# A graph-attention layer with its groups written out, its inputs laid out by partitions and its weights split by chunks

## What is computed

```python
h = jnp.maximum(_layernorm(x, axis=-1), 0.0)            # x: (64, 128, 384)
q = _heads(h @ Wq + bq)                                  # W: (384, 384), 6 heads of 64
k = _heads(h @ Wk + bk)
v = _heads(h @ Wv + bv)
scores = jnp.einsum('bhqd,bhkd->bhqk', q, k) / np.sqrt(HEAD_SIZE)
bias = jnp.where(adj, 0.0, NEG)[:, None]                 # adj: (64, 128, 128) booleans
probs = jax.nn.softmax(scores + bias, axis=-1)
ctx = jnp.einsum('bhqk,bhkd->bhqd', probs, v)
x = x + (ctx.transpose(0, 2, 1, 3).reshape(...) @ Wf + bf)
```

## Time and profile before

| | |
|---|---|
| median of three timed runs | 483.15 us (482.45 to 484.91) |
| the profiled execution's own time | 482.62 us |
| its span in the profile | 480.8 us |
| PE busy | 461.3 us, 96% |
| DVE busy | 366.4 us, 76% |
| ACT busy | 361.6 us, 75% |
| POOL busy | 304.3 us, 63% |
| moved by DMA | 79.76 MB |

### The profile page before, as it was taken

How to read it: one execution, slowest core, us unless ns; L and a number is a source line. 1 busy time by engine, 2 the same in 40 slices (tenths; PEclk the granted TensorE clock), 3 DMA queues, 4 the chain that set the end, 5 groups by cost and what they waited for, 6 DMA issues and landing times.

```text
span 480.8 us, 12961 instructions
## 1 busy us (share of the span) xinstructions
PE 461.3 (96%) x4451; PEld 272.9 (57%) x4451; DVE 366.4 (76%) x734; ACT 361.6 (75%) x806; POOL 304.3 (63%) x305
## 2 busy tenths in 40 slices
PE   6888989999999999999999999999999999999985
PEld 4644555646556564655656465565646565565643
DVE  3989878977769587776959777695977769477953
ACT  3478887877787887777788787778868778767850
POOL 4447665767757576776757677665767766654663
PEclk9999999999999999999999999999999999999999
DMA  7847597988989798686868869697997969756796
GB/s 245 177 66 152 108 191 158 154 189 135 221 118 205 166 168 207 129 221 131 202 144 178 191 131 219 132 204 149 172 198 127 222 116 165 168 117 147 144 188 182
DMA packets 231430, 79.76 MB, mean 166 GB/s; under 512 B 213331, under 2 KB 231382, under 8 KB 231382
## 3 DMA queue, kind: packets, MB, share of 16 engines
q1 hardware_dynamic: 214144, 66.09, 70.6%
q10 hardware_dynamic: 17238, 13.05, 10.4%
HBM read 16.19 MB, written 12.58 MB: 60 GB/s over the span
## 4 chain that ended last, share of the span: by engine, by line
PE 79%; DMA 7%; SPq 6%; DVE 3%; issue 2%; POOL 2%; ACT 1%; ACTq 0%; DVEq 0%
PE ps_proj L755 23%; PE ps_proj L757 22%; PE ps_proj L756 22%; PE ps_scores L828 6%; DMA ht_parts<-h_parts 3%; DMA ct_parts<-ctx_parts 2%; PE ps_ctx L755 2%; PE ps_ctx L756 2%; PE ps_ctx L757 2%; SPq L375 2%; SPq L359 2%; SPq L367 1%; DMA x_sb<-in_x 1%; DVE w_lo L690 1%; SPq L349 1%
## 5 line engine op out<-in xcount | busy, mean ns | idle before, releaser
L427 POOL TENSOR_TENSOR probs_parts<-probs,probs_parts 128x768 f16<-128x768 f32 x64 | 106.1, 1657 | 31.2 <-ACT probs_parts L519 30.3
L511 ACT ACTIVATE probs<-masked,neg_max 128x128 f32<-128x128 f32 x384 | 118.5, 390 | 0.2
L755 PE MATMUL ps_proj<-ht_parts,w_hi 128*128 128x512 f16 (+1 forms) x315 | 112.0, 361 | 5.3 <-DMA ht_parts<-h_parts 5.0
L756 PE MATMUL ps_proj<-ht_parts,w_hi 128*128 128x512 f16 (+1 forms) x315 | 111.9, 361 | 0.0
L757 PE MATMUL ps_proj<-ht_parts,w_lo 128*128 128x512 f16 (+1 forms) x315 | 111.9, 361 | 0.0
L491 ACT ACTIVATE qkt_hi<-ps_proj,bias_qk 128x512 f16<-128x512 f32 x96 | 65.3, 683 | 58.9 <-PE ps_proj L757 58.1
L412 POOL TENSOR_TENSOR h_parts<-h_sb,h_parts 128x384 f16<-128x384 f32 x64 | 58.9, 928 | 59.5 <-ACT h_sb L482 59.5
L590 DVE SCALAR_TENSOR_TENSOR qkt_lo<-ps_proj,bias_qk,qkt_hi 128x512 f16<-128x512 f32 x96 | 70.4, 741 | 29.7 <-ACT qkt_hi L491 29.7
L433 POOL TENSOR_TENSOR ctx_parts<-ctx_sb,ctx_parts 128x384 f16<-128x384 f32 x64 | 58.6, 915 | 51.6 <-ACT ctx_parts L525 51.1
L633 DVE SCALAR_TENSOR_TENSOR masked<-ps_scores,score_unscale,mask 128x384 f32<-128x384 f32 x128 | 72.6, 609 | 6.5 <-PE ps_scores L828 6.4
L422 POOL TENSOR_TENSOR x_bf<-x_sb,b_out 128x384 f32<-128x384 f32 x64 | 63.2, 999 | 9.8 <-DVE y_sb L663 8.8
(11 more groups left out here) (73 smaller groups left out, 887.6 us busy)
## 6 DMA issues: line engine op xcount, KB each, us to landing
y<-y_sb SPq DMA_DIRECT2D x64, 192.0 KB, 2.6
x_sb<-in_x ACTq DMA_DIRECT2D x60, 192.0 KB, 3.0
adj_sb<-in_adj ACTq DMA_DIRECT2D x16, 64.0 KB, 3.8
ht_parts<-h_parts SPq DMA_TRANSPOSE x64, 2.9
pt_parts<-probs_parts SPq DMA_TRANSPOSE x64, 4.0
ct_parts<-ctx_parts SPq DMA_TRANSPOSE x64, 2.5
x_sb<-in_x SPq DMA_DIRECT2D x4, 192.0 KB, 4.3
w_raw<-in_L_gnn_Wq SPq DMA_DIRECT2D x1, 576.0 KB, 7.8
```

The source lines that it names most:

```text
L427: nc.gpsimd.tensor_tensor(probs_parts[b][:, 1, :], probs[b % 2][:], probs_parts[b][:, 0, :], ALU.subtract).then_inc(probs_split, 1)
L511: last = nc.scalar.activation(probs[b % 2][:, u * N:(u + 1) * N], masked[b % 2][:, u, :], ACT.Exp, bias=neg_max[b % 2][:, u:u + 1])
L755: nc.tensor.matmul(to, a_hi, b_hi, start=first, stop=False)
L756: nc.tensor.matmul(to, a_hi, b_lo, start=False, stop=False)
```

## The change

All sixteen groups are written out; there is no loop on the engines. The tables of groups 0, 1, 14 and 15 have other turns (`TURNS` is the same), so the order changes in the first and last groups. The biases come from the host as one array of 128 by 3 by 3, so that one DMA brings them to their columns and PE no longer turns them; the mask's input is laid out by partitions, in runs of 512 B instead of 128 B. `bf` and the masks of groups 0 and 1 are loaded on SP's queue behind the weights, no longer on ACT's. `w_hi` and `w_lo` of the first three weights are written in three chunks, each with its own count of a semaphore, and PE waits chunk by chunk. `first_q` has its loops over chunks and tiles exchanged. `keep_busy` is called once with 20 instead of with 8 and 4.

```diff
-def run_turns(engine, stages):
-    todo = turns_of(stages)
-    for turn, stage, group, item in todo:
-        if turn < LOOP_TURNS[0]:
-            stages[stage](group, item, 0)
-    with engine.Fori(0, REPS) as i:
...
+def run_turns(stages):
+    for turn, stage, group, item in turns_of(stages):
+        stages[stage](group, item, 0)
...
     1: {
-        "statistics": (-65207, -58743, -57083, -46447), "aggregate": (-27850,), "inverse_deviation": (-60088,),
+        "statistics": (-28344, -20747, -20493, -13756), "aggregate": (-13197,), "inverse_deviation": (-20677,),
...
+            sp.dma_start(bf_rows[:], bf.partition_broadcast(P)).then_inc(bf_loaded, 16)
+            for n in range(2):
+                sp.dma_start(adj_sb[n][:], adj[n, :, :, :]).then_inc(adj_loaded[n], 16)
...
-            for n, bias in enumerate((bq, bk, bv)):
-                act.dma_start(bias_line[:, n, :], bias.rearrange("(o n) -> o n", o=1)).then_inc(bias_loaded, 16)
-            act.dma_start(bf_rows[:], bf.partition_broadcast(P)).then_inc(bf_loaded, 16)
-            act.wait_ge(consts_set, 5)
+            act.dma_start(bias_raw[:], biases).then_inc(bias_loaded, 16)
+            act.wait_ge(consts_set, 4)
             nc.scalar.activation(table_loader[:], eps[:], ACT.Exp)
-            load_mask(0, 0, 0)
-            act.wait_ge(bias_copied, 1)
...
-            load_mask(1, 0, 0)
+            for c in range(C):
+                weight_hi(1, slice(c, c + 1))
             for b in range(B):
                 load(1, b, 0)
-            weight_hi(1)
...
-                if group == 0 and j == 1:
-                    weight_hi(2)
+                if group == 0 and j == 2:
+                    for c in range(C):
+                        weight_hi(2, slice(c, c + 1))
...
-                if j == 0:
-                    scale(2)
...
                 if j == 2:
+                    for c in range(C):
+                        split_weight(2, slice(c, c + 1), c + 1)
+                if j == 5:
                     reduce_rows(3)
...
-            dve.wait_ge(bias_turned, 1)
-            nc.vector.tensor_copy(bias_raw[:], bias_turned_in.rearrange("p (n c) -> p n c", n=3))\
-                .then_inc(bias_copied, 1)
...
-            nc.vector.tensor_scalar(w_hi[0][:], w_raw[0][:], w_scale[:, 0:1], None, ALU.mult)\
-                .then_inc(w_hi_ready[0], 1)
-            split_weight(0)
+            for c in range(C):
+                chunk = slice(c, c + 1)
+                nc.vector.tensor_scalar(w_hi[0][:, chunk, :], w_raw[0][:, chunk, :], w_scale[:, 0:1], None, ALU.mult)\
+                    .then_inc(w_hi_ready[0], 1)
+                split_weight(0, chunk, c + 1)
...
             reduce_rows(2)
-            split_weight(1)
-            run_turns(dve, {
+            for c in range(C):
+                split_weight(1, slice(c, c + 1), c + 1)
+            scale(2)
...
                     pe.wait_ge(h_transposed[b], 16)
-                    if b == 0:
-                        pe.wait_ge(w_split, 1)
                     tokens = slice(b * N, (b + 1) * N)
-                    for j in range(C):
-                        at = slice(j * P, (j + 1) * P)
-                        for c in range(C):
+                    for c in range(C):
+                        if b == 0:
+                            pe.wait_ge(w_split[0], c + 1)
+                        for j in range(C):
+                            at = slice(j * P, (j + 1) * P)
...
-                    if b == 0:
+                    if b == 1:
                         sum_rows(1)
...
-            pe.wait_ge(consts_set, 5)
-            turn_biases()
-            keep_busy(8)
+            pe.wait_ge(consts_set, 4)
+            keep_busy(20)
             pe.wait_ge(bias_summed, 1)
             sum_rows(0)
             project_bias()
-            keep_busy(4)
```

More of the change, by code:

```diff
@@ L293, in build @@
         w_hi_ready = [sem(f"w_hi_ready{n}") for n in range(4)]
-        w_split = sem("w_split")
+        w_split = [sem(f"w_split{n}") for n in range(4)]
         biases_ready = sem("biases_ready")
@@ L502, in values_hi @@
                                      ACT.Copy).then_inc(v_hi_ready, 1)
-                if group == 0 and b == 1:
+                if group == 0 and b == B - 1:
                     weight_hi(3)
@@ L622, in values_lo @@
                                         v_hi[group % 2][:, b, :, 0:D], ALU.subtract).then_inc(v_split, 1)
-                if group == 0:
-                    between_first_values(b)
+                if group == 0 and b == 2:
+                    scale(3)
+                    dve.wait_ge(scale_step, 4 * SCALE_STEPS)
+                    nc.vector.tensor_tensor(y_unscale[:], w_unscale[:, 2:3], w_unscale[:, 3:4], ALU.mult)\
+                        .then_inc(unscales_ready, 1)
             def mask_scores(g, b, i):
@@ L787, in project_qk @@
                         pe.wait_ge(h_transposed[b], by_group(group, i))
-                if group == 0 and j == C:
-                    pe.wait_ge(w_split, 2)
                 ps = free_bank("project_qk", group, j, i)
@@ L793, in project_qk @@
                 for c in range(C):
+                    if group == 0 and j == C:
+                        pe.wait_ge(w_split[1], c + 1)
                     last = three_passes(ps[:], w_hi[w][:, c, at], w_lo[w][:, c, at], hi[:, c, :], lo[:, c, :],
@@ L806, in project_v @@
                 for c in range(C):
+                    if group == 0 and b == 0:
+                        pe.wait_ge(w_split[2], c + 1)
                     last = three_passes(ps[:, 0:H], hi[:, c, at], lo[:, c, at], w_hi[2][:, c, :], w_lo[2][:, c, :],
@@ L809, in project_v @@
                 last.then_inc(v_projected, 1)
+                if group == 0 and b == 2:
+                    sum_rows(3)
             def scores(g, pair, i):
@@ L870, in sum_rows @@
                 last.then_inc(rows_summed, 1)
-            def turn_biases():
-                pe.wait_ge(bias_loaded, 3 * 16)
-                for n in range(3):
-                    for c in range(C):
-                        k = C * n + c
-                        last = nc.tensor.matmul(bias_turned_in[:, k:k + 1], bias_line[:, n, c * P:(c + 1) * P], one[:],
-                                                start=True, stop=True)
-                last.then_inc(bias_turned, 1)
             def keep_busy(times):
@@ L900, in _, with laid_out @@
             project_bias()
-            keep_busy(4)
-            run_turns(pe, {
+            run_turns({
                 "project_qk": project_qk, "project_v": project_v, "scores": scores, "weigh_values": weigh_values,
                 "project_out": project_out})
-_INS = ["x", "adj", "L0_gnn_Wq", "L0_gnn_bq", "L0_gnn_Wk", "L0_gnn_bk", "L0_gnn_Wv", "L0_gnn_bv", "L0_gnn_Wf",
-        "L0_gnn_bf"]
+def laid_out(inputs, np):
+    adj = np.asarray(inputs["adj"]).reshape(GROUPS, B, N, N).transpose(0, 2, 1, 3)
+    biases = np.stack([np.asarray(inputs[f"L0_gnn_b{w}"]) for w in "qkv"]).reshape(3, C, P).transpose(2, 0, 1)
+    yield "x", inputs["x"]
+    yield "adj", adj
+    for w in "qkvf":
+        yield f"W{w}", inputs[f"L0_gnn_W{w}"]
+    yield "biases", biases
+    yield "bf", inputs["L0_gnn_bf"]
 def kernel(**inputs):
@@ L918 @@
     arrays, args = {}, []
-    for name in _INS:
-        a = _np.ascontiguousarray(inputs[name])
+    for name, a in laid_out(inputs, _np):
+        a = _np.ascontiguousarray(a)
         arrays[f"in_{name}"] = a
```

185 lines of the change are left out of this document (80 added, 105 removed).

## The result

The changed kernel took **487.53 us** (median of 9 runs, 482.63 to 490.83) against 483.15 of the kernel before: a ratio of 1.0064, 95% interval 1.0036 to 1.0092. Twelve more runs of it on another chip gave 484.84 against 483.39, 1.0024 (0.9996 to 1.0052). It is 0.2 to 0.6% slower where 1.4% less was forecast, and the second interval includes no change. Its profiled execution took 485.55 us, 2.93 more than the one of before.

What follows compares the result with a forecast made beforehand. PE was taken to bound the kernel, with only idle time at both ends to win. 4.3 + 2.3 = 6.6 us off the profiled 482.62 gave 476.0, with 0.53 for the median 476.5 us; range 472.5 to 480.7.

Steps and rivals of the forecast that it cites:

- Edits that cost nothing: Middle groups: writing out the loop, longer code and mask inputs in 512 B runs would each change the time by 0.
- The input queue: Beginning: with bf and masks behind the weights on SP's queue, 383 GB/s instead of 215; Wq's reduction at about 6.3 us.
- First matmul at 12.95: Beginning: earlier input landings let PE start its first real matmul at 12.95 instead of 16.50, gaining 3.5 us.
- First Q products end at 19.4: Group 0: the four graphs' first projections run nearly without a gap until 19.4 us, where it was 23.7.
- the rival to which I gave 0.13: Beginning: PE's clock falls in a new 2.7 us pause before the first matmul, losing 1.7 us, giving 478.2; chance 0.13.
- Group 1 at 38.4: PE begins group 1 at 38.4 instead of 41.58, a gain of 3.2 us with bounds 1.5 and 4.6.
- group 1's loads come late: Beginning: loads behind w_hi chunks land too late, the gain is lost, 486 or so; row sum slips over 8 us; chance 0.06.
- Group 2's wait gone: Before group 2: inputs land at 61.4, most of the 1.6 us wait goes, 1.1 gained; 4.3 us in all there.
- The end, 2.3 us: Last groups: the new order ends PE at 474.8 to 475.5 instead of 477.8; 2.3 us, bounds 0 and 4.9.
- Sum: Whole kernel: 4.3 us up to group 2 plus 2.3 at the end, 6.6 us off, giving 476.5 us.

Runs made afterwards that it cites:

- unroll_only: The kernel before with its loop written out and nothing else: 483.94 us, ratio 0.9985.
- fill_both: The changed kernel with 11 warming matmuls ahead of the first Q products and 15 ahead of group 1: 484.21 us, ratio 1.0004.
- the second run: The changed kernel itself, unaltered, run twelve more times on another chip: 484.84 us, ratio 1.0024.
- early_g1: The changed kernel with group 1's x loaded before the split of Wk, its statistics, shift and two normalizations earlier: 484.39 us, ratio 0.9995.
- the whole chain: The changed kernel with early Wk row sums and group 1's loads, statistics, shift, normalizations ahead, behind group 0's transposes: 482.77 us (0.9977), again 484.94 (1.0025).

## Why the prediction was wrong, point by point

- **Edits that cost nothing: right.** Middle groups are 27.97 us again, unroll_only is level.
- **The input queue: right in kind.** 283 GB/s from 3 to 8 us where I wanted over 300, and 388 after. Wq's reduction began at 8.31, not 6.3: the rate was short of my 383 in this stretch, and x of graph 2 landed only at 5.77.
- **First matmul at 12.95: 14.74.** A gain of 1.8 in place of 3.5 us. The first transpose was issued at 9.41 (8.5 forecast) and took 5.28 us behind the weights. (I also had PE's `keep_busy` of before start at 3.7 us. That was the turning of the biases, and `keep_busy` started at 7.64; nothing in the sum hangs on it.) The six chunks of Wq took 4.4 us and not 2.9 to 3.3 (the middle pair 1.07 and 1.35 beside POOL's subtractions, the last 0.41 and 0.62), so the last was ready at 15.1.
- **First Q products end at 19.4: 22.67.** 1.8 from the start and 1.5 from the clock. This was the rival to which I gave 0.13: the pause of 2.54 us is the one I had named, and the cost where it stands, 1.6 us against fill_both, is near the 1.7 us I had priced. The Trainium skill's page "TensorE: Matmul & The Clock Gate" (HAM oscillation — how this bites in real kernels) tells of a matmul kernel in which each wait for a DMA makes the next tile start slow. The rows here agree for the longest pauses (all seven of 3.2 to 5.0 us were followed by a fall), and show in the two runs of the changed kernel that a pause of 2.5 us may do it or not.
- **Group 1 at 38.4: 43.63. This is the step that failed.** Its forecast was DVE's scale of Wk done at 16.9, the shift at 28.2, SP's last issue at 34.6 and a landing of 2.9 to 4.1 us. Measured: 20.21, 31.28, 38.14 and 5.24. The 3.3 us at the scale are the late start (1.8) and the slow clock (1.5); the row sums behind the second graph were in the forecast. They go through the chain nearly whole, and the landing adds 1 to 2 us. In the second run's trace, without the slow clock, the shift is done at 29.42 and the last transpose issued at 36.82, and a landing of 6.03 us still brings group 1 to 43.10. So two terms were too small in both traces, the time of the first matmul, on which all of DVE's chain hangs, and the landing. Loads of the next groups were issued beside it, at 36.16 to 41.06 us; that they made it slow is argued from early_g1, not shown for this transpose. The slower rival, "group 1's loads come late", priced the way by the loads, which landed at 25.10 (its 24.5) while DVE only came to their statistics at 26.53: DVE's order was the limit and not the loads. It asked for over 8 us of slip of the row sum where 3.3 were enough. The runs show what the order is worth: the row sums moved ahead give back 1.3 us, the whole chain 4.8.
- **Group 2's wait gone: right by luck.** PE found group 2's inputs ready, as forecast, but they landed at 68.34 where I had 61.4. PE itself came late, at 69.40 for 61.5.
- **A second fall of the clock**, behind the pause ahead of group 1, was in no case of mine: 2.7 us. I priced one pause, and not those that a late input makes.
- **The end, 2.3 us: 0.1.** The first scores of the last pair did come earlier relative to group 13 (57.7 us after it, 59.2 before), but PE waited 3.6 us for ct_parts (2.9 before): one of these transposes took 4.64 us from issue to landing, where I had counted 3.20. That comes out at my lower bound of 0.
- **Sum.** 6.6 us forecast. Measured in the profiled executions: 1.2 gained to the first scores, 2.05 lost at group 1, 3.1 at group 2, 2.9 at PE's end.

## What to carry to other kernels

An early start only counts as far as the next group's inputs come earlier too: follow the chain of the second group from the moved instruction to its last landing before pricing the first. Where a change opens a pause on TensorE, price the slow matmuls behind it as well, and look at the granted clock of many executions. Compare kernels at equal clock too: a ratio of 0.9975 shrank to 0.6 us that way, and one of 1.0021 grew to 2.1 us. Idle matmuls in four of the longest pauses of the changed kernel kept its clock, but a fixed number of them can run past the landing that it waits for. A load moved away from transposes speeds them up, but it has to be put somewhere where its own reader isn't the next bottleneck.

## What the runs showed of the hardware that I had not expected

- In the 20 traces, all seven pauses of 3.2 to 5.0 us on TensorE have a fall to 1.2 GHz during them or within 1 us behind. Of the 32 pauses of 2.1 to 2.9 us 17 have one within 1.5 us, and the same pause of the same kernel has it in one execution and not in another (2.54 and 2.58 us in the two runs of the changed kernel). No shorter pause has one. A fall in the last 20 us, each time at a pause of 2.1 to 2.7 us, is in 7 of the 14 traces with the new end and in 1 of the 6 with the old one; the stretch from group 13 to the end then takes 87.1 to 89.3 us, otherwise 85.3 to 86.9.
- A transpose by DMA (128 x 768 float16) took 2.7 us at best, and 6.4 to 10.4 us beside four loads of 192 KB on the other queue (group 0's in early_g1 and the two kernels built on it).
- In the changed kernel's trace VectorE's two operations on a chunk of Wq took 1.07 and 1.35 us while GpSimd subtracted, and 0.41 and 0.62 us on another chunk when it didn't. That one caused the other is argued from this coincidence only.
